# Router steps dealt out singly between low parts, router products one tile later, and idle products in waits: a four-layer gated mixture kernel on one core

## Chip, cores and metric

The kernel runs on one core of a Trainium2 chip. The metric is device time in microseconds (us) of one execution; lower is better.

## What is computed

Four layers update a residual stream x of 8 x 128 tokens by 128 features. Each layer adds a gated cross attention to 77 context tokens and then a gated feed-forward part. Three of the feed-forward parts (layers 0, 1 and 3) are mixtures of 8 experts with the two best experts of each token; layer 2 is a block-quantised feed-forward part. The part of layer 1 that the change touches most, cut from the reference:

```
nx = _ln(x, ln_g, ln_b)
logits = nx @ router_w
probs = jax.nn.softmax(logits, axis=-1)
_, idx = jax.lax.top_k(probs, K)
mask = jnp.sum(jax.nn.one_hot(idx, probs.shape[-1], dtype=probs.dtype), axis=1)
w = probs * mask
w = w / jnp.sum(w, axis=-1, keepdims=True)
h1 = _gelu(jnp.einsum('th,ehf->etf', nx, up_W) + up_b[:, None, :])
...
s0 = _gelu(_ln(jnp.einsum('etf,efg->etg', h1[i0], spec0_W) + spec0_b[:, None, :], ln0_g[:, None, :], ln0_b[:, None, :]))
...
out_e = jnp.einsum('etf,efh->eth', h2, down_W) + down_b[:, None, :]
y = jnp.einsum('eth,te->th', out_e, w) + x
```

Layer 3's mixture is the same without the inner products: relu of an up product, a down product, a softmax over the two kept logits.

## The kernel before

All engines run programs written out by hand, with semaphores between them. The tokens are handled in two halves h of 512. A float32 product is made of three products of rounded parts (`mm3`): an operand is split into a high part (fp32r, by ScalarE) and a low part (the difference, by VectorE for activations, line 1188, and by GpSimd for weights, line 647; the weights' high parts `WH` are ScalarE's, line 737). So every result of an up, inner or turned product in PSUM is read twice by ScalarE (lines 843 and 846) and once by VectorE (`H1l`, `H2l`, the "low parts"), and only after the low part may TensorE use it.

`plan()` writes one list of jobs per mixture (`order[0]`, `order[1]`, `order[3]`); each engine walks that list in `mixture()` and does its share of each job, so the list sets the order on all engines at once. `weave(a, b, ...)` merges lists, list number i starting i rounds later. Up, inner (`spec0`), turned (`turn`), weight (`wgt`) and `spread` results go through a ring of six PSUM banks: TensorE waits, six jobs later, for the reader of that bank (in layer 1 the VectorE low part, in layer 3 ScalarE). Down products accumulate in PS4 and PS5.

Names at the start of layer 1's mixture: four up jobs of expert 0 half 0 (u0 to u3), then four `spec0` jobs (here s0 to s3: a bias row `ROWr` and four groups of three products, one group for each low part of u0 to u3), each followed on VectorE by moments (line 1138) and a scaling `SN` (line 1146). Between them stand held-over steps of the attention part: `late_scale` (ScalarE, line 753, four `XN` tiles), `late_stats` (VectorE), `late_norm` (GpSimd, then ScalarE's four `XM` tiles), and `second`: TensorE turns the second half of XM (line 1504) into XT, ScalarE copies it twice (XT, XTh), VectorE makes XTl (line 1048), and TensorE multiplies it by the router (`logits`, 16 short product instructions of 8 columns, out<-in `PS<-RW,XT`).

The routing itself is VectorE work on 64 numbers per partition (`route`, lines 1065 to 1107): in five parts, part 0 from the logits to the exponent's argument, part 1 the softmax, parts 2 and 3 the two picks, part 4 the weights `WG` and their three bf16 parts `WGS`. `WGS` is turned by TensorE (`wgt`), copied by ScalarE (`WGT`) and spread over the partitions.

After s0 to s3 of the second half come the turned tiles of half 0 (t0 to t3) and of half 1 (r0 to r3), with two up jobs of expert 1 (n0, n1) between them and two more (n2, n3) and the down products of half 1 (e0 to e3) behind them.

`keep_clock(n)` issues n products that nobody reads (`PS<-MB,identb`, 512 columns, bf16).

Of the kernel before, what the change touches and what calls it, by code (L numbers as in the profile page):

```python
# [10 lines left out]
E = 8  # L11
HALF = 512
TH = HALF // S
# [26 lines left out]
def plan():  # L40
# [18 lines left out]
    for p in range(E0P):  # L59
        b = p * U0COLS  # L60
# [38 lines left out]
    route = lambda: [dict(kind="route", part=k) for k in range(5)]  # L99
    second = [dict(kind="second")]  # L100
    order = {0: [], 1: [], 3: []}
# [4 lines left out]
    for n in range(len(x) + 2):  # L106
# [4 lines left out]
        if n == 0:  # L111
            k = route()
            order[0] += k[0:1] + a[0:2] + k[1:2] + a[2:3] + k[2:3] + a[3:4] + k[3:4] + more
        elif n == 1:
            order[0] += a[0:1] + k[4:5] + weave(a[1:], b, c, more)
# [44 lines left out]
    o += u[0:1] + chain("late_scale") + u[1:2] + chain("late_stats") + u[2:4] + chain("late_norm") + s[0:2] + second  # L160
    wq = [dict(kind="quantise", layer=1, i=i, k=k) for i in range(7) for k in range(9)]
    for e in range(E):
# [43 lines left out]
    for n in range(len(x) + 2):  # L206
# [71 lines left out]
def program(nc, a, out):  # L278
# [48 lines left out]
    with ctx:  # L327
# [403 lines left out]
        def _(act):  # L731
# [46 lines left out]
            def mixture(n, layer):  # L778
                for s_ in ORDER[layer]:
                    kind = s_["kind"]  # L780
                    if kind in ("split", "quantise", "down", "down0", "spec0", "spec1b", "weigh") or kind in HELD:
# [15 lines left out]
                    if kind == "route":  # L797
                        if s_["part"] == 0:
                            gate(n)
                        continue  # L800
# [197 lines left out]
        def _(dve):  # L998
# [54 lines left out]
            def route(n, layer, part):  # L1053
# [5 lines left out]
                if part == 0:  # L1059
# [11 lines left out]
                elif part == 1:  # L1071
                    dve.wait_ge(gate_exp, n + 1)
                    if layer < 3:

                        now(v.tensor_reduce(RM[:, 1, :], rt3(1), AX.X, ALU.add))
                        now(v.reciprocal(RM[:, 2, :], RM[:, 1, :]))
                        now(v.tensor_tensor(rt3(2), rt3(1), per_token(RM, 2), ALU.mult))
                elif part in (2, 3):

                    pick = part - 2  # L1080
                    scores = 7 if pick else (9 if layer == 3 else 2)
                    now(v.tensor_reduce(RM[:, 0, :], rt3(scores), AX.X, ALU.max))
                    now(v.tensor_tensor(rt3(3), rt3(scores), per_token(RM, 0), ALU.is_equal))
                    now(v.tensor_tensor(rt(4), rt(3), rev, ALU.mult))
# [932 lines left out]
```

## Time and profile before

| | |
|---|---|
| median of 3 runs (lowest to highest) | 724.83 us (722.32 to 725.20) |
| the profiled execution | 724.68 us |
| its span, first to last instruction | 722.9 us |
| mean granted TensorE clock | 0.964 of full speed |
| busy: TensorE, VectorE, ScalarE, GpSimd | 656.1, 479.8, 436.7, 182.7 us |

The span and the 1.8 us around it make the execution's time. Layer 1's mixture runs from about 181 to 477 us of the span, layer 2 from 477 to 541 us, layer 3's attention from 541 to 604 us and its mixture from 609 to 719 us.

### The profile page before, as it was taken

The page shows a single profiled execution, that of the slowest core. Times are in us where ns is not written, and L with a number is a line of the kernel's source. Part 1 is how long each engine was busy: PE and PEld are TensorE (multiplying, and loading weights), DVE is VectorE, ACT ScalarE, POOL GpSimd, SP SyncE. Part 2 cuts the span into 40 slices and gives each one's busy share as a digit, 9 for nine tenths or more (in the row PEclk, how much of TensorE's full clock was granted, in tenths as well). Part 3 has the DMA queues.
Part 4 walks back from the last instruction along what each step waited for, and adds up shares of the span by engine and source line. Part 5 has one row for each costly group of instructions (what it writes and reads, how often), then busy time and mean ns, then how long its engine had stood idle before and what let it go on. Part 6 is the DMA issues. An engine that isn't in the chain of part 4 may idle for free.

```text
span 722.9 us, 10213 instructions
## 1 busy us (share of the span) xinstructions
PE 656.1 (91%) x3563; PEld 478.1 (66%) x3573; DVE 479.8 (66%) x1093; ACT 436.7 (60%) x820; POOL 182.7 (25%) x215
## 2 busy tenths in 40 slices
PE   4889999998799799998999999997799997889997
PEld 1589996565466677776767667765555665667775
DVE  2477674587447567359657684368975763669996
ACT  4457454877436667668358486655127664877773
POOL 3414000541124033224241512041013001124531
PEclk9789999999789999999999999999999999999999
DMA  5112002020002000022010110010001000110001
GB/s 137 52 31 63 1 1 73 2 88 2 0 2 75 12 15 30 1 73 84 19 59 16 29 60 1 1 47 0 1 1 58 2 3 0 30 46 14 1 0 30
DMA packets 27361, 20.98 MB, mean 29 GB/s; under 512 B 5409, under 2 KB 22571, under 8 KB 27311
## 3 DMA queue, kind: packets, MB, share of 16 engines
q1 hardware_dynamic: 26591, 20.29, 9.3%
q8 instruction: 29, 0.48, 0.3%
q14 instruction: 21, 0.17, 0.1%
q10 hardware_dynamic: 720, 0.04, 0.1%
HBM read 19.80 MB, written 0.52 MB: 28 GB/s over the span
## 4 chain that ended last, share of the span: by engine, by line
PE 62%; DVE 17%; ACT 13%; issue 5%; POOL 2%; DMA 1%; ACTq 0%; DVEq 0%; POOLq 0%
PE PS L1483 54%; ACT PS L846 3%; PE PS L1723 2%; ACT H2h L843 2%; PE PS L1589 2%; ACT H1h L843 2%; ACT XN L753 1%; DVE ST L1020 1%; DVE H2l L1188 1%; DMA GW<-in_L_gate_T 1%; PE PS L1745 1%; PE PS L1504 1%; DVE ATT L1276 1%; ACT WH L737 1%; DVE H1l L1188 1%
## 5 line engine op out<-in xcount | busy, mean ns | idle before, releaser
L647 POOL TENSOR_TENSOR WL<-RAW,WH 128x512 fp32r<-128x512 f32 (+2 forms) x76 | 89.2, 1189 | 147.5 <-ACT WH L737 147.2
L1188 DVE TENSOR_TENSOR H2l<-PS,H2h 128x512 fp32r<-128x512 f32 x72 | 49.3, 689 | 57.9 <-ACT PS L846 57.4
L737 ACT ACTIVATE ATT<-PS 77x512 f32<-77x512 f32 (+5 forms) x92 | 46.7, 533 | 33.6 <-PE PS L1927 15.7
L639 POOL TENSOR_TENSOR RSTD<-VE,MHALF 128x4 f32<-128x4 f32 x18 | 18.6, 1032 | 185.1 <-DVE VE L1030 149.4
L1483 PE MATMUL PS<-XTh,WH 128*128 128x512 f32 x128 | 54.5, 426 | 11.0 <-DVE XTl L1048 4.1
L1483 PE MATMUL PS<-H1h,WH 128*128 128x512 f32 x146 | 60.2, 412 | 2.2 <-DVE H1l L1188 2.2
L665 POOL TENSOR_TENSOR XT<-XT,YW 128x512 f32<-128x512 f32 x24 | 32.2, 1342 | 113.1 <-DVE YW L1125 113.1
L1483 PE MATMUL PS<-H1l,WH 128*128 128x512 f32 x146 | 57.2, 392 | 0.0
L1483 PE MATMUL PS<-H1h,WL 128*128 128x512 f32 x146 | 57.1, 391 | 0.0
L1483 PE MATMUL PS<-XTl,WH 128*128 128x512 f32 x128 | 52.6, 411 | 0.0
L1483 PE MATMUL PS<-XTh,WL 128*128 128x512 f32 x128 | 52.6, 411 | 0.0
L1483 PE MATMUL PS<-H2h,WH 128*128 128x512 f32 (+1 forms) x108 | 48.5, 449 | 2.9 <-DVE H2l L1188 2.2
L1268 DVE TENSOR_REDUCE MX<-PS 128x4 f32<-128x308 f32 x64 | 30.2, 474 | 31.1 <-PE PS L1483 30.7
L843 ACT ACTIVATE H1h<-PS,UB 128x512 fp32r<-128x512 f32 x48 | 33.9, 707 | 26.3 <-PE PS L1483 26.1
L1483 PE MATMUL PS<-MB,identb 128*128 128x512 bf16 (+1 forms) x192 | 48.4, 369 | 0.9 <-issue 0.5
L1188 DVE TENSOR_TENSOR H1l<-PS,H1h 128x512 fp32r<-128x512 f32 x48 | 32.9, 689 | 19.7 <-ACT PS L846 19.4
L846 ACT ACTIVATE PS<-PS,UB 128x512 f32<-128x512 f32 x64 | 44.1, 688 | 0.0
L846 ACT ACTIVATE G<-PS,FB 128x512 f32<-128x512 f32 x64 | 42.6, 704 | 2.0 <-PE PS L1483 0.9
L843 ACT ACTIVATE H2h<-PS,SB 128x512 fp32r<-128x512 f32 x24 | 16.5, 689 | 44.0 <-PE PS L1483 44.0
L1483 PE MATMUL PS<-H2l,WH 128*128 128x512 f32 (+1 forms) x108 | 42.5, 394 | 0.0
L1483 PE MATMUL PS<-H2h,WL 128*128 128x512 f32 (+1 forms) x108 | 42.4, 393 | 0.0
L737 ACT ACTIVATE WH<-RAW 128x512 fp32r<-128x512 f32 (+2 forms) x76 | 41.5, 589 | 0.0
(254 smaller groups left out, 1651.0 us busy)
## 6 DMA issues: line engine op xcount, KB each, us to landing
RAW<-in_L_ffn_spec_W SPq DMA_DIRECT2D x4, 1024.0 KB, 5.5
RAW<-in_L_ffn_w SPq DMA_DIRECT2D x16, 256.0 KB, 3.0
RAW<-in_L_ffn_up_W SPq DMA_DIRECT2D x8, 256.0 KB, 2.7
RAW<-in_L_ffn_down_W SPq DMA_DIRECT2D x8, 256.0 KB, 3.4
RAW<-in_L_ffn_spec1a_W SPq DMA_DIRECT2D x2, 512.0 KB, 4.3
RAW<-in_L_ffn_spec1b_W SPq DMA_DIRECT2D x2, 512.0 KB, 5.6
RAW<-in_L_ffn_wg SPq DMA_DIRECT2D x4, 176.0 KB, 2.6
RAW<-in_L_ffn_wu SPq DMA_DIRECT2D x4, 176.0 KB, 2.7
```

What stands on the lines that cost most here:

```text
L639: step(g.tensor_tensor(RSTD[:, c], VE[:, c], MHALF[:, c], ALU.pow))
L647: g.tensor_tensor(lo, RAW[0:r["rows"], r["raw"] + s["c0"]:r["raw"] + s["c1"]], hi.bitcast(fp32), ALU.subtract).then_inc(lo_done, 1)
L665: g.tensor_tensor(y, y, YW[:, (d % 2) * HALF:(d % 2 + 1) * HALF], ALU.add).then_inc(y_added, 1)
L737: return s.activation(o, i, ACT.Copy)
L753: s.activation(dst[:, t, :], src[:, t, :], ACT.Identity, scale=RSTD[:, t:t + 1], bias=NMR[:, t:t + 1]).then_inc(xn_ready, 1)
L843: s.activation(HID[s_["buf"]][0][:, i * HALF:(i + 1) * HALF], bank[:, :], func, bias=bias, scale=scale)
L846: s.activation(full, bank[:, :], func, bias=bias, scale=scale).then_inc(act_freed, 1)
L1188: v.tensor_tensor(lo, full, hi.bitcast(fp32), ALU.subtract).then_inc(split_done, 1)
L1268: v.tensor_reduce(MX[:, (g % 4) * GH:(g % 4 + 1) * GH], bank(g), AX.X, ALU.max).then_inc(max_done, 1)
L1483: return t_.matmul(o, l, r, start=start, stop=stop)
L1589: last = t_.transpose(o[0:rows, t * S:(t + 1) * S], SN[:, s["slot"], at:at + rows], ident[:, :])
L1723: last = t_.transpose(PS[3 + g % 2][0:KC, m * S:(m + 1) * S], group(PB, g)[:, m * KC:(m + 1) * KC], ident[:, :])
```

## The change

The routing is cut into single steps k = 0 to 25 instead of five parts, and `dealt(items, more, per)` puts `per` of them behind each job. In layer 0 the slices give the same VectorE order as before. In layer 1 the steps go behind the s, t, weight and r jobs, two at a time, then one at a time; in layer 3 behind the up jobs and the jobs of the next round, three at a time. `late_scale` stands two up jobs later; the router products are a job of their own (`scores`), one `spec0` tile behind the turning. Layer 3 puts the second half's turning and its copies ahead of the weight splits of that round, and drops an empty list from every `weave` of layer 3, so that down products and weight splits start one round earlier. Idle products are added in layer 1 (7, before the last group of s0), in layer 3 (6, before the router products) and in layer 2 (9 instead of 8 around the stream products, with half of the context products moved behind the turning; 12, 12, 14, 18 instead of 10, 6, 10, 18 in the feed-forward part).

```
-    route = lambda: [dict(kind="route", part=k) for k in range(5)]
+    route = lambda layer: [dict(kind="route", k=k) for k in range(26)
+                           if not (layer == 0 and k >= 22 or layer == 3 and k in (2, 3))]
     second = [dict(kind="second")]
+    scores = [dict(kind="scores")]
+
+    def dealt(items, more, per):
+
+        out = []
+        for s in items:
+            out.append(s)
+            out += more[:per]
+            more = more[per:]
+        return out, more
...
-            k = route()
-            order[0] += k[0:1] + a[0:2] + k[1:2] + a[2:3] + k[2:3] + a[3:4] + k[3:4] + more
+            k = route(0)
+            order[0] += k[0:1] + a[0:2] + k[1:4] + a[2:3] + k[4:11] + a[3:4] + k[11:16] + more
...
-    o += u[0:1] + chain("late_scale") + u[1:2] + chain("late_stats") + u[2:4] + chain("late_norm") + s[0:2] + second
+    o += u[0:3] + chain("late_scale") + u[3:4] + chain("late_stats", "late_norm") + s[0:2] + second + s[2:3] + scores
...
-            o += weave(s[2:] if e == 0 else spec("spec0", 0, TH), up(e, 1), new[:4])
-            k = route() if e == 0 else []
+            o += weave(s[3:] if e == 0 else spec("spec0", 0, TH), up(e, 1), new[:4])
+            k = route(1) if e == 0 else []
             o += k[0:1]
-            o += weave(spec("spec0", 1, TH), spec("turn", 0, 4, buf=2, hi="act"), new[4:], k[1:])
-            o += nxt[:1] + weave(spec("turn", 1, 4, buf=3, hi="act"), down(e, 0), nxt[1:2])
+            u, k = dealt(weave(spec("spec0", 1, TH), spec("turn", 0, 4, buf=2, hi="act"), new[4:]), k[1:], 2)
+            o += u
+            u, k = dealt(nxt[:1] + weave(spec("turn", 1, 4, buf=3, hi="act"), down(e, 0), nxt[1:2]), k, 1)
+            o += u + k
             o += weave(nxt[2:], down(e, 1))
...
-        order[3] += weave(a, {1: route()[1:3], 2: route()[3:]}.get(n, []), c, more)
         if n == 0:
-            order[3] += second + route()[0:1]
+            r = route(3)
+            order[3] += a + second + scores + more
+        elif n == 1:
+            order[3] += r[0:1] + a[0:2] + r[1:3] + a[2:3] + r[3:5] + a[3:4] + r[5:7]
+        elif n == 2:
+            a, r = dealt(weave(a, c, more), r[7:], 3)
+            order[3] += a + r
+        else:
+            order[3] += weave(a, c, more)
...
+                    if kind == "scores":
+                        k, w = (3, RW1) if layer == 1 else (7, RW3)
+                        if layer == 3:
+                            keep_clock(6, PS[4])
                         logits(n, w[:, :], k)
                         continue
...
+                            if e == 0 and h == 0 and i == 0 and f == nf - 1:
+                                keep_clock(7, PS[4])
...
             context_part(0)
+            keep_clock(7)
+            turn(4, *normed(5, XN), halves=(0,))
             context_part(1)
-            keep_clock(4)
-            turn(4, *normed(5, XN), halves=(0,))
-            keep_clock(4)
+            keep_clock(2)
             stream_part(0)
...
-                keep_clock((10, 6, 10, 18)[p])
+                keep_clock((12, 12, 14, 18)[p])
```

The first place is the start of layer 1's mixture on ScalarE. Before, the four `XN` tiles (`late_scale`) stand behind the first up job:

```order
L843 ACTIVATE H1h<-PS,UB 128x512
L846 ACTIVATE PS<-PS,UB 128x512
L753 ACTIVATE XN<-X,NMR,RSTD 128x128 x4
L843 ACTIVATE H1h<-PS,UB 128x512
L846 ACTIVATE PS<-PS,UB 128x512
```

Now they stand behind the third:

```order
L863 ACTIVATE H1h<-PS,UB 128x512
L866 ACTIVATE PS<-PS,UB 128x512
L863 ACTIVATE H1h<-PS,UB 128x512
L866 ACTIVATE PS<-PS,UB 128x512
L863 ACTIVATE H1h<-PS,UB 128x512
L866 ACTIVATE PS<-PS,UB 128x512
L773 ACTIVATE XN<-X,NMR,RSTD 128x128 x4
```

Two up results are read two jobs earlier, and the four tiles come behind them. On TensorE at the same place the turning, the router products and s2 stood like this before:

```order
L1504 MATMUL PS<-ident,XM 128x128 x4
L1483 MATMUL PS<-RW,XT 128x8 x8
L1483 MATMUL PS<-ROWr,onesr 128x512
L1483 MATMUL PS<-WH,H1h 128x512
L1483 MATMUL PS<-WL,H1h 128x512
```

Now, with the seven idle products ahead of the last group of s0, and the router products behind s2:

```order
L1518 MATMUL PS<-MB,identb 128x512 x7
L1518 MATMUL PS<-WH,H1h 128x512
...
L1539 MATMUL PS<-ident,XM 128x128 x4
L1518 MATMUL PS<-ROWr,onesr 128x512
...
L1518 MATMUL PS<-RW,XT 128x8 x8
L1518 MATMUL PS<-ROWr,onesr 128x512
```

The second place is VectorE in layer 1, from the low part of t2 to that of n0 (the one `H1l` row). Before, 22 of the 25 routing steps behind the exponent stand between t3's low part and n0's (the first two and the last two are shown):

```order
L1188 TENSOR_TENSOR H2l<-PS,H2h 128x512
L1082 TENSOR_REDUCE RM<-RT 128x8
L1083 TENSOR_TENSOR RT<-RT,RM 128x64
...
L1106 CAST WGS<-RT 128x8x8
L1107 TENSOR_TENSOR WGS<-RT,WGS 128x8x8
L1188 TENSOR_TENSOR H1l<-PS,H1h 128x512
L1188 TENSOR_TENSOR H2l<-PS,H2h 128x512 x3
```

Now the low parts of t2, t3 and n0 stand between them, and thirteen of the steps are ahead of t2:

```order
L1223 TENSOR_TENSOR H2l<-PS,H2h 128x512
L1115 TENSOR_TENSOR RT<-RT,RM 128x64
L1119 TENSOR_TENSOR RT<-RT 128x64
L1121 TENSOR_TENSOR RT<-RT 128x64
L1123 TENSOR_REDUCE RM<-RT 128x8
L1223 TENSOR_TENSOR H2l<-PS,H2h 128x512
L1127 RECIPROCAL RM<-RM 128x8
L1129 TENSOR_TENSOR RT<-RT,RM 128x64
L1223 TENSOR_TENSOR H1l<-PS,H1h 128x512
L1131 TENSOR_SCALAR WG<-RT,TG 128x64
```

Two steps stand between t3's low part and n0's where there were 22. The third place is ScalarE at the start of layer 3's mixture. Before, two weight splits stand ahead of the copies of the second half's turned tiles:

```order
L846 ACTIVATE G<-PS,FB 128x512
L737 ACTIVATE WH<-RAW 128x512 x2
L737 ACTIVATE XT<-PS 128x512
L737 ACTIVATE XTh<-PS 128x512
L927 ACTIVATE RT<-RT 128x64
```

Now behind them:

```order
L866 ACTIVATE G<-PS,FB 128x512
L757 ACTIVATE XT<-PS 128x512
L757 ACTIVATE XTh<-PS 128x512
L757 ACTIVATE WH<-RAW 128x512 x2
L947 ACTIVATE RT<-RT 128x64
```

The copies are issued two splits earlier, and so the splits' high parts, which GpSimd waits for, two copies later.

## Rows read from the trace of the kernel before

**Rows 1.** Windows: length, busy us of PE, PEld, DVE, ACT, POOL; clock; DMA.
```profile
180.80:189.40 8.60, 5.18 (x22) 3.31 (x20) 4.53 (x19) 6.35 (x12) 1.21 (x2) 1.00 0.00 1
189.40:199.60 10.20, 9.14 (x20) 6.14 (x20) 3.57 (x12) 2.44 (x6) 1.75 (x3) 0.50 0.00 0
203.00:206.40 3.40, 3.40 (x10) 2.65 (x9) 0.17 (x1) 0.00 (x0) 0.00 (x0) 0.50 0.00 0
240.60:244.00 3.40, 3.08 (x7) 2.48 (x8) 3.32 (x7) 1.99 (x4) 0.00 (x0) 0.50 0.00 0
482.90:486.30 3.40, 3.38 (x10) 1.80 (x11) 0.31 (x1) 2.83 (x8) 3.32 (x5) 0.50 0.00 0
```

**Rows 2.** Timeline, start of layer 1: start, length, engine, [idle before <-releaser].
```profile
182.37 0.65 ACT L846 ACTIVATE PS<-PS,UB 128x512 f32<-128x512 f32 x1
185.13 1.65 ACT L753 ACTIVATE XN<-X,NMR,RSTD 128x128 f32<-128x128 f32 x4 [2.10 <-POOL NMR L640]
188.66 0.50 PE L1483 MATMUL PS<-WH,H1h 128*128 128x512 f32 x1 [3.26 <-DVE H1l L1188]
190.78 0.80 PE L1483 MATMUL PS<-WH,H1h 128*128 128x512 f32 x1 [1.05 <-DVE H1l L1188]
191.47 1.65 ACT L753 ACTIVATE XM<-XN,NMR,RSTD 128x128 f32<-128x128 f32 x4 [1.28 <-POOL NMR L640]
200.08 2.09 PE L1483 MATMUL PS<-RW,XT 128*128 128x8 f32 x16
207.07 0.49 PE L1483 MATMUL PS<-ROWr,onesr 33*128 33x512 f32 x1
210.36 0.40 PE L1483 MATMUL PS<-XTh,WH 128*128 128x512 f32 x1
```

**Rows 3.** Timeline, layer 1 around the routing.
```profile
234.03 0.68 ACT L846 ACTIVATE PS<-PS,UB 128x512 f32<-128x512 f32 x1
234.32 0.21 DVE L1082 TENSOR_REDUCE RM<-RT 128x8 f32<-128x64 f32 x1
239.95 0.23 DVE L1107 TENSOR_TENSOR WGS<-RT,WGS 128x64 bf16<-128x64 f32 x1
240.37 0.84 ACT L846 ACTIVATE PS<-PS,LB,LG 128x512 f32<-128x512 f32 x1
240.92 0.77 PE L1483 MATMUL PS<-XTh,WH 128*128 128x512 f32 x1 [3.01 <-DVE H1l L1188]
248.10 0.60 PE L1483 MATMUL PS<-WGT,PICK 96*128 96x512 bf16 x2 [0.95 <-ACT WGT L737]
```

**Rows 4.** Timeline, layer 2.
```profile
484.58 0.60 ACT L737 ACTIVATE XT<-PS 128x512 f32<-128x512 f32 x1 [0.57 <-PE PS L1504]
487.35 0.75 DVE L1238 SCALAR_TENSOR_TENSOR X<-PS,TG,X 128x512 f32<-128x512 f32 x1 [4.14 <-PE PS L1483]
519.04 0.87 PE L1927 MATMUL PS<-ident,ATT 128*128 128x128 f32 x6 [1.62 <-DVE ATT L1355]
```

**Rows 5.** Timeline, start of layer 3's mixture.
```profile
616.02 1.18 ACT L737 ACTIVATE WH<-RAW 128x512 fp32r<-128x512 f32 x2
616.76 2.49 POOL L647 TENSOR_TENSOR WL<-RAW,WH 128x512 fp32r<-128x512 f32 x2 [10.69 <-ACT WH L737]
618.21 1.59 DVE L1048 TENSOR_TENSOR XTl<-XT,XTh 128x512 fp32r<-128x512 f32 x1 [1.32 <-ACT XTh L737]
619.90 0.76 PE L1483 MATMUL PS<-XTh,WH 128*128 128x512 f32 x1 [1.10 <-POOL WL L647]
638.71 0.61 PE L1483 MATMUL PS<-WGT,PICK 96*128 96x512 bf16 x2 [2.27 <-ACT WGT L737]
```

**Rows 6.** Line 1188 on DVE: nanoseconds, least, median, most; first and last start.
```profile
L1188 DVE TENSOR_TENSOR H1l<-PS,H1h x48: 678/691/694, 183.7 to 449.2; 128x512 fp32r<-128x512 f32 x48
L1188 DVE TENSOR_TENSOR H1l<-G,H1h x32: 677/692/1783, 612.6 to 700.6; 128x512 fp32r<-128x512 f32 x32
```

**Rows 7.** Windows, layer 3's mixture in full flow, columns as in Rows 1.
```profile
656.00:700.00 44.00, 44.00 (x190) 34.15 (x189) 43.49 (x53) 34.12 (x59) 21.43 (x14) 1.00 0.00 1
```

More of the change, by code:

```diff
@@ L111, in plan @@
         if n == 0:
-            k = route()
-            order[0] += k[0:1] + a[0:2] + k[1:2] + a[2:3] + k[2:3] + a[3:4] + k[3:4] + more
+            k = route(0)
+            order[0] += k[0:1] + a[0:2] + k[1:4] + a[2:3] + k[4:11] + a[3:4] + k[11:16] + more
         elif n == 1:
-            order[0] += a[0:1] + k[4:5] + weave(a[1:], b, c, more)
+            order[0] += a[0:1] + k[16:] + weave(a[1:], b, c, more)
         elif n == E0P + 2:
@@ L780, in mixture @@
                     kind = s_["kind"]
-                    if kind in ("split", "quantise", "down", "down0", "spec0", "spec1b", "weigh") or kind in HELD:
+                    if kind in ("split", "quantise", "scores", "down", "down0", "spec0", "spec1b", "weigh") or kind in HELD:
                         if kind == "y_copy":
@@ L797, in mixture @@
                     if kind == "route":
-                        if s_["part"] == 0:
+                        if s_["k"] == 0:
                             gate(n)
@@ L1051, in per_token, with route @@
                 return m[:, row, :].rearrange("p (t o) -> p t o", o=1).to_broadcast([128, B, E])
-            def route(n, layer, part):
+            def route(n, layer, k):
                 rt = lambda i: RT[:, i, :]
@@ L1058, in route @@
                 prob = 1 if layer == 3 else 2
-                if part == 0:
+                third = lambda k: WGS[:, :, 32 * k:32 * k + E]
+                wg = WG[:, :].rearrange("p (t e) -> p t e", e=E)
+                if k == 0:
                     dve.wait_ge(v1_ready, 1)
@@ L1070, in route @@
                     v.tensor_tensor(rt3(0), rt3(9), per_token(RM, 0), ALU.subtract).then_inc(dif_ready, 1)
-                elif part == 1:
+                elif k == 1:
                     dve.wait_ge(gate_exp, n + 1)
@@ L1095, in route @@
                     now(v.reciprocal(RM[:, 1, :], RM[:, 0, :]))
+                elif k == 20:
                     now(v.tensor_tensor(rt3(8), rt3(8), per_token(RM, 1), ALU.mult))
+                elif k == 21:
                     v.tensor_scalar(WG[:, :], rt(8), tg(4 + layer), None, ALU.mult).then_inc(wg_ready, 1)
                     dve.wait_ge(wg_ready, n + 1)
[L1099 to L1107 removed]
+                elif k == 22:
+                    now(v.memset(WGS[:, :, :], 0.0))
+                    now(v.tensor_copy(third(0), wg))
+                elif k == 23:
+                    now(v.tensor_tensor(rt3(8), wg, third(0), ALU.subtract))
+                elif k == 24:
+                    now(v.tensor_copy(third(1), rt3(8)))
+                else:
+                    v.tensor_tensor(third(2), rt3(8), third(1), ALU.subtract).then_inc(wgs_ready, 1)
             def mixture(n, layer):
@@ L1153, in mixture @@
                     if kind == "route":
-                        route(n, layer, s["part"])
+                        route(n, layer, s["k"])
                     elif kind == "second":
```

43 lines of the change are left out of this document (23 added, 20 removed).

## The prediction, as put on record before the changed kernel ran

> **What bounds the kernel now.** I read the windows first, then the waits in the timeline, place by place. TensorE is busy 656.1 of 722.9 us, so time is to be had only where it waits, or where it runs at 1.2 GHz instead of 2.4. The windows show such stretches [rows 1]: 189.4 to 199.6, 203.0 to 206.4, 240.6 to 244.0 and 482.9 to 486.3 stand at 0.50. The reader is to see that each follows a wait or a stretch of short products, and that a stretch full of products (9.14 busy of 10.20) still runs at half rate once it has fallen.
>
> The waits, in order of time. In layer 1, TensorE has the first group of s0 done and waits 3.26 us for the low part of u1, then 1.05 for those of u2 and u3 [rows 2]. The releaser is VectorE, but the late one is ScalarE: behind u0 (its last read starts 182.37) it stands at the four `XN` tiles until NMR is there, 185.13, and is done with them at 186.78; only then does it read u1. Around the routing, TensorE waits 3.01 us for n0's low part, at 240.92. ScalarE had n0 read at 234.03 + 0.68 = 234.71, so VectorE is late by itself: 22 routing steps run from 234.32 to 240.18 ahead of it [rows 3]. That is 5.86 us, 0.266 us a step. In layer 3's mixture TensorE waits for XTl, which VectorE made in 1.59 us, from 618.21 to 619.80, though the row of TensorE names GpSimd [rows 5]. In the flow of layer 3 TensorE is busy all 44.00 us [rows 7], and in layer 2's feed-forward part the waits before line 1927 are for VectorE's quantising [rows 4].
>
> **The change, term by term.** A product group of 512 columns goes by every 0.23 us at full clock. I take a whole `spec0` tile from rows: 207.07 to 210.36, 3.29 us for 13 products [rows 2].
>
> *A, start of layer 1.* ScalarE reads 512 columns every 0.59 us (two in 1.18 [rows 5]), so an up result takes 1.2. u0 is done at 183.0, then u1 at 184.2 and u2 at 185.3; NMR comes at 185.1, so the tiles move by only 0.2 (185.3 to 186.9), and u3 is read at 188.1. VectorE's low parts (0.69 each [rows 6]) are then there at about 185.0, 186.0 and, for u3, 188.8. TensorE does groups two and three of s0 by 186.8, the seven idle products (7 x 0.23 = 1.6) by 188.4, and starts the last group at 188.9: 189.6. Then s1 with 3.29: 192.9. The turning needs XM. `late_stats` follows u3's low part, 0.2 later than before, so the XM tiles end at 191.47 + 1.65 + 0.2 = 193.3 and the turning at 193.5 [rows 2]. s2: 196.8, and the router products, 2.0 of their 2.09 behind it: 198.8. At that point the old kernel, with s2 and the router products behind it as well, stood at 207.07. The gain is 8.2 us if the clock stays at 2.4 GHz. Ahead of the fall TensorE was busy 5.18 of 8.60 us, with the 3.26 wait in it [rows 1]; of that wait 0.5 is left, which makes about 7.9, so I expect the long slow stretch gone. But the short slow one, 203.0 to 206.4, came directly behind the turning and the router products, at a time when TensorE had no wait at all. The same products are still issued, so I keep that stretch and charge half of its 3.4 us: **A = -6.5**. Ends: -8.2 without it; -4.2 if the 10.2 us stay slow (s1 6.0 at half rate until 195.5, the turning to 195.7, s2 3.9 slow and 1.2 fast to 200.8, router 202.9).
>
> The Trainium skill bears on this ("TensorE: Matmul & The Clock Gate", Part 4: PE-mode transpose): transposes do not count as busy in the way other products do. By that the fall behind the turning stays; by the row of 203.0 alone it is the router products or the turning. Both say 1.7 us are still paid.
>
> *B, the routing in layer 1.* Thirteen steps move into VectorE's idle time ahead of t2's low part. Six run between t2's and n0's low parts and cost 6 x 0.266 = 1.6 us, against 25 (6.6) before. So n0's low part ends at about 236.3, not 240.8, and TensorE, which began to wait at 240.92 - 3.01 = 237.9, goes on at once, and without the stretch at 0.50 that came of it. What is late next is ScalarE: it reads r3 until 240.37 + 0.84 = 241.2, then n2 and n3 (2 x 1.2), then makes the two WGT copies (1.2): 244.8. The products with WGT start there instead of at 248.10 [rows 3]: **B = -3.3**. Ends: -4.6 (the whole wait and half of 3.4 slow us); -1.0 if routing steps ahead of t0's to t3's low parts hold TensorE's ring.
>
> *C, layer 2.* XT is there at 485.18; the stream products stood behind four idle products at half rate, and their VectorE reader started at 487.35 [rows 4]. Now a half of the context products (1.0) and two idle ones (0.45) stand behind the turning: reader at about 486.75 if the clock is full, -0.6; at half rate about 488.6, +1.3. Whether the granted clock stays is not to be read from these rows, as TensorE is equally busy ahead of it. **C = 0**. The idle products in the feed-forward part lie in waits: six more at line 1927's second wait are 1.4 us in 1.62 [rows 4]; VectorE, which sets the pace there, does not wait for them. If the clock fell there, 12 products would take 5.1 us and be late by about 2.
>
> *D, layer 3's start.* Without the two weight splits (1.18 us [rows 5]) ahead, ScalarE makes XT and XTh by 617.1. GpSimd's low parts of the weights, which ran from 616.76 to 619.25 over XTl, come later, so XTl takes 0.69 and is ready at 617.9 instead of 619.80. The six idle products (1.4) and the router products lie in the old wait (done 617.7). Next up job: 618.0, not 619.90, which is -1.9. Its first three products took half rate (0.76 and so on, where 210.36 has 0.40); at full clock ScalarE has its first result another 0.7 sooner, -2.6. Ahead of the last low part of the third round nine routing steps stand now instead of twelve, 3 x 0.27 more, -3.4. The 2.27 wait for the WGT copies [rows 5], which are ScalarE's, stays. Between these I take **D = -3.0**, ends -1.9 and -3.7.
>
> *The rest.* Layer 0's VectorE order is the same: 0. In layer 3's flow the down products stand one place earlier, but they use low parts two rounds old, and ScalarE's splits only change places: 0.
>
> Sum: -6.5 - 3.3 + 0 - 3.0 = -12.8. From the profiled execution, 724.68 (span 722.9 and 1.8 around it; the median is 724.83, the same within 0.15): 711.9, so **712 us**.
>
> The contention in D is also a rule: the Trainium skill ("GPSIMD Engine Reference", 1. Specifications) lists SBUF access as shared with VectorE, with contention when its instruction has two SBUF inputs. The low parts agree: from PSUM never over 694 ns in 48, from `G` in SBUF up to 1783 [rows 6]. The routing steps have two SBUF inputs as well. So this rule speaks against the change in one respect, the next rival but one.
>
> **Rivals.** *The clock does not hold in layer 1* (0.14). For it: full stretches stayed at 0.50 once [rows 1]; against: the wait that preceded them goes. A is then -4.2: 714.2.
>
> *The waits come back* (0.13): routing steps ahead of low parts delay TensorE's ring in layer 1 (B = -1.0) and the last low part of the third round in layer 3 (nine steps stand ahead of it, D = -1.9): 715.3. For it: each step stands in an in-order queue; against: the steps are the same in sum and only begin earlier.
>
> *Slower: VectorE becomes the bound in layer 3's flow* (0.03). It is busy 43.49 of 44.00 us there [rows 7], with low parts stretched to 1.78 beside GpSimd. Down products earlier and splits between up jobs change which of its instructions meet GpSimd's. The flow is seven pairs of rounds; it has 0.5 us of slack in 44. If in each pair three more of its eight low parts stretch by 1.1 (0.69 to 1.78), that is 3.3 a pair, 23.1 in all, less about 0.9 of slack: 712 + 22.2 = 734. It decides from 2 us a pair on (7 x 2 - 0.9 = 13). Against: the order of VectorE and GpSimd is the same there.
>
> *The skill's rule on the port* (0.08): in layer 3 the last nine steps meet the two low weight parts (2.5 us of GpSimd). They would end 2.5 later and take D to -0.5: 714.5. The page is the one named above, and the rule agrees with the 1.59 of XTl.
>
> *More than forecast* (0.10): the slow stretch behind the router products goes, A -8.2 instead of -6.5, and C at -0.6: 709.7.
>
> **How the numbers follow.** The forecast itself has 0.52, at 710 to 714. The range 707.5 to 717.5 takes in all the best ends together (-8.2 - 4.6 - 0.6 - 3.7 is 707.6) and all rivals but the slower one; it leaves about 0.15 out. A change of 0.5% (3.6 us) is about what a measurement of this kernel can tell from none: under 721.2 is faster. The cases there hold 0.93; 0.04 for two or three terms failing together, 0.03 for the slower rival.
>
> **What would show it.** Right: in layer 1 no wait over 1 us between the first and last group of s0, granted clock 1.00 through s1, 8 us less from u0's first product to s3 give or take 2; no wait for n0's low part, and the products with WGT bounded by ScalarE, 3.3 us earlier; XTl of 0.7 us in layer 3; VectorE's waits none in layer 2's feed-forward part. Wrong: a slow stretch over s1 and s2, waits for `H2l` on TensorE between t0 and r3, any wait of TensorE in layer 3's flow, or new slow stretches elsewhere that give back 1.7 us each.

## The result and the profile after

The changed kernel takes 718.01 us (median of 4, 717.73 to 719.47), the kernel before 724.68 in the same comparison. The ratio is 0.9924, 95% interval 0.9899 to 0.9949: 6.7 us faster, where 12.7 had been forecast, and just outside the forecast's range (707.5 to 717.5). The profiled execution took 719.47 us with a span of 717.7.

The windows of the changed kernel, columns as in [rows 1]:

```profile
186.00:199.00 13.00, 12.64 (x59) 8.61 (x59) 8.38 (x25) 4.48 (x9) 3.34 (x5) 1.00 0.00 0
199.00:202.40 3.40, 3.40 (x9) 2.62 (x10) 0.47 (x1) 0.00 (x0) 0.00 (x0) 0.50 0.00 0
226.30:229.70 3.40, 2.84 (x11) 2.65 (x12) 3.20 (x9) 3.07 (x6) 0.90 (x1) 0.50 0.63 211
328.70:332.10 3.40, 3.40 (x10) 2.63 (x9) 3.16 (x9) 2.38 (x4) 0.85 (x1) 0.50 0.69 231
506.20:509.60 3.40, 3.40 (x14) 3.15 (x15) 3.23 (x6) 0.38 (x2) 0.00 (x0) 0.50 0.02 5
629.10:639.30 10.20, 7.31 (x17) 5.11 (x18) 4.41 (x8) 5.10 (x10) 0.00 (x0) 0.50 0.00 1
```

The 10.2 us at half clock in layer 1 [rows 1] are gone: 186 to 199 us stand at 1.00. But the stretch at 328.7 is new, and in layer 3 there are 10.2 us from 629.1 where the kernel before has 3.4 (from 639.9). In layer 3's flow, 650 to 694 us, TensorE is busy all 44.00 us as in [rows 7], so the rival that made the kernel slower did not come. The timeline of the changed kernel, with the waits in brackets:

```profile
188.17 0.50 PE L1518 MATMUL PS<-WH,H1h 128*128 128x512 f32 x1 [0.18 <-DVE H1l L1223]
198.48 0.49 PE L1518 MATMUL PS<-ROWr,onesr 33*128 33x512 f32 x1
221.46 1.29 POOL L667 TENSOR_TENSOR WL<-RAW,WH 128x512 fp32r<-128x512 f32 x1 [0.60 <-ACT WH L757]
221.69 1.14 DVE L1115 TENSOR_TENSOR RT<-RT,RM 128x64 f32<-128x64 f32 x1
224.23 0.70 DVE L1173 BATCH_NORM_STATS2 ST<-PS 128x6 f32<-128x512 f32 x1
226.86 1.97 PE L1682 MATMUL PS<-ident,SN 128*128 128x128 f32 x8 [2.50 <-DVE SN L1181]
233.49 0.39 PE L1518 MATMUL PS<-XTh,WH 128*128 128x512 f32 x1
328.31 0.50 PE L1518 MATMUL PS<-XTh,WH 128*128 128x512 f32 x1 [2.02 <-POOL WL L667]
611.35 0.69 DVE L1068 TENSOR_TENSOR XTl<-XT,XTh 128x512 fp32r<-128x512 f32 x1 [0.28 <-ACT XTh L757]
627.51 0.65 PE L1518 MATMUL PS<-identb,WGS 128*96 128x128 bf16 x8 [1.05 <-DVE WGS L1142]
630.43 1.03 PE L1518 MATMUL PS<-WGT,PICK 96*128 96x512 bf16 x2 [2.27 <-ACT WGT L757]
635.59 0.77 PE L1518 MATMUL PS<-H2h,WH 128*128 128x512 f32 x1 [1.55 <-DVE XT L1160]
```

The waits for u1 and n0 are gone. In their place stand 2.50 us for the scaled tile SN, and in layer 3 1.55 us for VectorE's weighing into XT (the step that reads a finished down product out of PS4 and multiplies it by the gate weights). At these two places the timeline of the kernel before has 1.09 and 0.38:

```profile
232.47 1.09 PE L1640 MATMUL PS<-ident,SN 128*128 128x128 f32 x8 [1.09 <-DVE SN L1146]
...
642.92 0.67 PE L1483 MATMUL PS<-H2h,WH 128*128 128x512 f32 x1 [0.38 <-DVE XT L1125]
```

Since the first product of layer 1's mixture starts anywhere from 179.9 to 182.7 us in these traces, whatever was edited, the traces are compared by the lengths between five marks on TensorE: u0's first product (M0), the first `spec0` product of the second half (M1), the WGT products of layer 1 (M2), the first up product of layer 3 (M3), the WGT products of layer 3 (M4), and the end of TensorE's last instruction (M5). The starts are read from each run's timeline and subtracted; us:

```
run                   M0-M1  M1-M2   M2-M3  M3-M4  M4-M5   median  ratio to before (95%)
before                32.47  34.83  361.55  29.06  80.69
the change            26.06  32.95  364.51  26.73  83.73   718.01  0.9924 (0.9899-0.9949)
l3_list_back          26.07  32.97  364.51  26.13  81.90   716.98  0.9893 (0.9867-0.9920)
l1_route_old          26.07  34.80  362.94  26.74  83.71   720.46  0.9934 (0.9909-0.9958)
l1_no_idle            25.57  33.23  362.90  26.65  82.75   718.11  0.9912 (0.9889-0.9935)
l2_old                26.13  33.09  363.27  26.63  81.87   718.18  0.9913 (0.9891-0.9936)
before_late_scale     28.81  34.99  361.60  29.06  80.74   719.02  0.9926 (0.9906-0.9945)
list_back_no_idle     25.58  33.18  362.85  26.25  81.49   716.52  0.9880 (0.9858-0.9903)
plus_no_idle_l3       28.66  33.21  362.92  27.29  80.48   716.98  0.9894 (0.9873-0.9916)
plus_deal_later       25.57  31.96  362.72  24.61  80.48   715.22  0.9864 (0.9833-0.9895)
before_A_alone        26.07  34.94  361.61  29.07  80.67   718.54  0.9936 (0.9912-0.9959)
before_B_alone        32.49  33.25  363.20  29.07  80.70   724.27  1.0013 (0.9997-1.0029)
before_D_alone        32.54  34.90  361.54  26.00  80.70   721.10  0.9963 (0.9947-0.9979)
before_list_dropped   29.73  34.92  361.55  28.82  82.75   727.52  1.0055 (1.0035-1.0075)
before_B_shifted      32.44  34.65  361.63  29.05  80.73   724.54  1.0008 (0.9993-1.0024)
before_B_later        32.72  31.96  363.10  29.31  80.50   720.86  0.9966 (0.9944-0.9989)
parts_best            25.58  31.94  361.67  26.00  80.66   712.18  0.9850 (0.9827-0.9874)
```

The ratios are each to the kernel before as it ran in the same comparison. Its median was 724.68 us there for the change, 724.76 for the next eight lines, 723.67 for the four from `before_A_alone` on and 723.93 for the last three, so medians of different groups are not to be subtracted to a few tenths. The lengths are those of one profiled execution each. One of the nine executions of `l1_route_old` took 816.09 us at a granted clock of 0.754 and is left out of its ratio.

By the first two lines the change gained 6.4 (A), 1.9 (B) and 2.3 us (D), and lost 3.0 between M2 and M3 and 3.0 behind M4.

### The profile page after: what moved, and what is told of

Its sections match the earlier page's. It is cut to its first block, busy times and chain, and to the rows that moved or that the text cites. A ratio compares the mean times of both kernels' runs of the same rounds, so it can differ in the third digit from the quotient of the medians.

```text
span 717.7 us, 10278 instructions
## 1 busy us (share of the span) xinstructions
PE 660.7 (92%) x3588; PEld 480.7 (67%) x3599; DVE 481.4 (67%) x1093; ACT 438.7 (61%) x820; POOL 183.1 (26%) x215
## 4 chain that ended last, share of the span: by engine, by line
PE 64%; DVE 16%; ACT 13%; issue 4%; POOL 2%; DMA 1%; ACTq 0%; DVEq 0%; POOLq 0%
PE PS L1518 55%; ACT PS L866 3%; PE PS L1765 3%; ACT H2h L863 2%; PE PS L1629 2%; ACT H1h L863 2%; ACT XN L773 1%; DVE H2l L1223 1%; PE PS L1787 1%; DVE ST L1040 1%; PE PS L1682 1%; DMA GW<-in_L_gate_T 1%; DVE QS L1363 1%; PE PS L1539 1%; ACT ATT L757 1%
## 5 line engine op out<-in xcount | busy, mean ns | idle before, releaser
L1518 PE MATMUL PS<-MB,identb 128*128 128x512 bf16 (+1 forms) x217 | 54.4, 372 | 1.0 <-issue 0.5
L1223 DVE TENSOR_TENSOR H1l<-PS,H1h 128x512 fp32r<-128x512 f32 x48 | 32.9, 689 | 18.5 <-ACT PS L866 18.3
L1518 PEld LDWEIGHTS PS<-MB,identb 128*128 128x128 bf16 x228 | 20.2, 101 | 34.4 <-issue 20.4
```

The costliest lines, as they stand in the source:

```text
L1223: v.tensor_tensor(lo, full, hi.bitcast(fp32), ALU.subtract).then_inc(split_done, 1)
L1518: return t_.matmul(o, l, r, start=start, stop=stop)
```

## The experiments

**Undoing one edit of the change.** `l3_list_back` puts layer 3's empty list back:

```diff
-            a, r = dealt(weave(a, c, more), r[7:], 3)
+            a, r = dealt(weave(a, [], c, more), r[7:], 3)
...
-            order[3] += weave(a, c, more)
+            order[3] += weave(a, [], c, more)
```

> The changed kernel with one edit undone: the empty list is back in layer 3's weaves, so that down products and weight splits start one round later, as before. Theory 1 (the earlier first down product waits for the weighing of the accumulator it writes over, and the wait and the low clock with it give back what the start of layer 3 gained): the wait of 1.55 us on DVE XT is gone or under 0.5, the stretch at clock 0.50 in layer 3's third round is 3.4 us instead of 10.2, and the time is 2.5 to 3 us under the changed kernel, 715.2 (before is 724.7). Rival (the low clock comes from the 2.27 us wait for the WGT copies alone, and falls wherever that stands): the stretch stays 10.2 us long, and the time falls by at most 1 us, to 717 or more.

716.98. The wait for XT is 0.28 us, as theory 1 said, but the stretch at half clock is 6.8 us long, not 3.4, and 1.0 us was gained by the median where 2.8 was expected; that is the time the rival named, and the two intervals overlap. In the profiled runs M3 to M4 is 0.6 and M4 to M5 1.8 shorter. Theory 1 has the direction, not the size, and the 0.28 is no proof of its cause, as `plus_deal_later` shows below.

`l1_route_old` puts layer 1's routing back into the four blocks of before:

```diff
-            u, k = dealt(weave(spec("spec0", 1, TH), spec("turn", 0, 4, buf=2, hi="act"), new[4:]), k[1:], 2)
-            o += u
-            u, k = dealt(nxt[:1] + weave(spec("turn", 1, 4, buf=3, hi="act"), down(e, 0), nxt[1:2]), k, 1)
-            o += u + k
+            parts = [k[1:4], k[4:11], k[11:16], k[16:]] if k else []
+            for s in weave(spec("spec0", 1, TH), spec("turn", 0, 4, buf=2, hi="act"), new[4:], parts):
+                o += s if isinstance(s, list) else [s]
+            o += nxt[:1] + weave(spec("turn", 1, 4, buf=3, hi="act"), down(e, 0), nxt[1:2])
```

> The changed kernel with layer 1's routing in the four blocks of before. Theory 1 (dealing out is worth little there, 1.8 us, since a step that meets GpSimd's weight split takes 1.14 us instead of 0.22 and moves the scaling SN of the last tile): 719.8, with a wait of about 3 us for n0's low part and none over 1.5 us at the turned tiles. Rival (it is worth the 3.3 us forecast and the loss is elsewhere): 721.3. Second rival (it is worth nothing; either way one wait and one stretch at clock 0.50): 718.

M1 to M2 is 34.80, 1.85 us more than with the dealing, and the 3.01 us wait for n0 is back. But M2 to M3 is 1.6 us shorter: no stretch at half clock stands behind the wait for WL. 720.46 lies between theory 1 and the rival, but its runs (716.07 to 722.32, the one of 816.09 apart) take in those of the change, and the ratios can't be told apart. In the traces B's gain is real and smaller than forecast, and something later takes most of it.

`l1_no_idle` drops the seven idle products:

```diff
-                            if e == 0 and h == 0 and i == 0 and f == nf - 1:
-                                keep_clock(7, PS[4])
```

> The changed kernel without the seven idle products ahead of the last group of s0 in layer 1. Theory 1 (the shorter wait is what keeps the clock, the idle products do nothing): same time as the changed kernel, 718, clock 1.00 from 186 to 198 us. Rival (they keep the clock): TensorE waits 1.6 us there, a stretch at 0.50 of 3.4 to 10.2 us follows through s1 and s2, and the time is 719.7 to 722.5.

The total stays, 718.11, yet not by theory 1's way: TensorE waits 1.72 us, and a stretch of 3.4 us comes at 190.1, but the one of 199.0 does not. M0 to M1 is 0.5 us shorter than with them. The idle products only moved where the clock falls. (Of four later runs with the same start of layer 1 three show 25.6 us for that part and one 28.66, with 6.8 us of half clock from 189.9 and 3.4 more behind the router products, so the fall can also be longer.)

`l2_old` undoes part C:

```diff
             context_part(0)
-            keep_clock(7)
-            turn(4, *normed(5, XN), halves=(0,))
             context_part(1)
-            keep_clock(2)
+            keep_clock(4)
+            turn(4, *normed(5, XN), halves=(0,))
+            keep_clock(4)
...
-                keep_clock((12, 12, 14, 18)[p])
+                keep_clock((10, 6, 10, 18)[p])
```

> The changed kernel with layer 2 as before: both halves of the context products ahead of the turning, 4 and 4 idle products, and 10, 6, 10, 18 in the feed-forward part. Theory 1 (the order behind the turning costs 1.1 us at the half clock: two idle products and half of the context products stand ahead of the stream products, and six more idle ones behind them): 716.9, and VectorE's second addition to X comes 3.6 us behind its first instead of 4.7. Rival (the place of the low clock decides, not the order): within 0.5 us of the changed kernel, 718.

The second addition to X comes 3.6 us behind the first, as theory 1 said (481.68 and 485.26; in the changed kernel 480.25 and 484.97). The time does not follow: 718.18. The rival holds in the median, though the profiled run is 1.2 us shorter between M2 and M3 than that of the change.

**A first combination.** `before_late_scale` is the kernel before with one line:

```diff
-    o += u[0:1] + chain("late_scale") + u[1:2] + chain("late_stats") + u[2:4] + chain("late_norm") + s[0:2] + second
+    o += u[0:3] + chain("late_scale") + u[3:4] + chain("late_stats", "late_norm") + s[0:2] + second
```

> The kernel before with one edit of the change: late_scale two up jobs later (and late_stats with late_norm behind the fourth). No idle products, router products where they were, routing in blocks. Theory 1 (the shorter wait alone keeps TensorE's clock through s1 and s2): from u0's first product to the second half's first products 26 to 27 us instead of 32.5, one stretch of 3.4 us at clock 0.50 there instead of 10.2 and 3.4, and 718.5. Rival (the router products behind s2 are needed too): the stretch of 10.2 us stays and only the waits go, 721 to 722.

719.02, ratio 0.9926: this line alone gives as much as the whole change (0.9924). Theory 1 holds for the size; in the profiled run, which is the longest of the five (720.87), the stretch is 6.8 us long with 3.4 behind the router products (28.81, not 26 to 27).

`list_back_no_idle` is `l3_list_back` without the seven idle products.

> The changed kernel with the empty list back in layer 3 and without layer 1's seven idle products. Theory 1 (the two act in stages far apart and add up: -1.0 as measured for the list, -0.5 for layer 1's start by the stretch from u0 to the second half, 25.6 us against 26.1): 716.5. Rival (a removal of 0.5 us moves everything behind it against the clock's stretches, so that sums do not hold): anything from 715 to 719, with the stretches at 0.50 at other places than in the two runs apart.

716.52, as theory 1 said.

`plus_no_idle_l3` is that without the six idle products ahead of layer 3's router products:

```diff
-                        if layer == 3:
-                            keep_clock(6, PS[4])
```

> As list_back_no_idle, and without the six idle products ahead of layer 3's router products. Theory 1 (they do nothing for the clock, and lie in a wait): the same time within 0.5 us. Rival (they keep the clock): the stretch at 0.50 around the router products grows by 3.4 us or more and costs 1 to 2 us between the first up product and the WGT products of layer 3 (26.1 to 26.7 us so far).

716.98, within 0.5 us, as theory 1 said. But in the profiled run M3 to M4 is 1.0 longer and 6.8 us of half clock stand at the router products (from 613.2), where the run without this edit has none; that is what the rival named. The runs of 716.5 to 718.9 overlap those without the edit (714.5 to 717.3). Whether the six idle products help is not settled.

`plus_deal_later` deals layer 1's steps otherwise:

```diff
-            u, k = dealt(weave(spec("spec0", 1, TH), spec("turn", 0, 4, buf=2, hi="act"), new[4:]), k[1:], 2)
-            o += u
-            u, k = dealt(nxt[:1] + weave(spec("turn", 1, 4, buf=3, hi="act"), down(e, 0), nxt[1:2]), k, 1)
+            k = k[1:]
+            for s in weave(spec("spec0", 1, TH), spec("turn", 0, 4, buf=2, hi="act"), new[4:]):
+                o.append(s)
+                if s["kind"] != "split" and (s["kind"], s["i"]) != ("turn", 1):
+                    o += k[:2]
+                    k = k[2:]
+            u, k = dealt(nxt[:1] + weave(spec("turn", 1, 4, buf=3, hi="act"), down(e, 0), nxt[1:2]), k, 2)
             o += u + k
```

> As list_back_no_idle, with layer 1's routing dealt out otherwise: no steps behind t1 and behind weight splits, so that the moments of the last spec0 tile stand four to six steps earlier on VectorE, and two steps instead of one behind the jobs that follow t3. Theory 1 (the steps ahead of the last tile's moments, one of them stretched to 1.14 us beside GpSimd, cause TensorE's 2.50 us wait for SN and the low clock with it): the wait is 1.1 us as in the kernel before, and the time from the second half's first product to the WGT products is 31.3 us instead of 33.0; 715. Rival (the steps only move: n0's or r0's low part is late instead): the wait for SN is shorter and waits of the same sum stand at the H1l and H2l behind it; 33 us, 716.5.

M1 to M2 is 31.96, 1.2 us shorter than in `list_back_no_idle`, and no stretch stands there. 715.22, as theory 1 said, but with runs from 711.7 to 719.1. The waits went the rival's way: 1.73 us for SN instead of 2.50 (not 1.1), and a new one of 0.83 for a low part behind it, 2.56 together. So the 1.2 us are the stretch at half clock that did not come, not a shorter wait. TensorE's timeline:

```profile
226.51 1.09 PE L1684 MATMUL PS<-ident,SN 128*128 128x128 f32 x8 [1.73 <-DVE SN L1185]
236.26 0.50 PE L1522 MATMUL PS<-H2h,WH 128*128 128x512 f32 x1 [0.83 <-DVE H2l L1227]
630.14 0.47 PE L1522 MATMUL PS<-H2h,WH 128*128 128x512 f32 x1 [1.49 <-DVE XT L1164]
```

The last row stands in layer 3, where this kernel has the empty list: the wait for XT is 1.49 us and not 0.28. It is as long in `plus_no_idle_l3`, which has the list too, and in `before_B_later`, whose layer 3 is that of the kernel before. What the three share is full clock between the WGT products and this one. The product starts 4.20 us behind the WGT products here, 4.21 in the kernel before and 4.20 in `before_list_dropped`: in these three VectorE's weighing sets that time, with and without the list. With a stretch at half clock there, TensorE's three groups of up products fill the wait; at full clock they leave 1.49 us.

**One part at a time on the kernel before.** `before_A_alone` has `late_scale`, the idle products and `scores` as in the change, `before_B_alone` the dealing in layer 1, `before_D_alone` layer 3's start with the empty list kept; their edits are those lines of the change, with the routing steps and the router products that are not under test in their old places. `before_list_dropped` drops the empty list, with the routing's blocks still behind the second and third up job (`b0`, `b1`):

```diff
-        order[3] += weave(a, {1: route()[1:3], 2: route()[3:]}.get(n, []), c, more)
...
+            order[3] += weave(a, c, more) + second + scores + r[0:1]
...
+            order[3] += flat(weave([a[0], a[1:2] + b0, a[2:3] + b1, a[3]], c, more))
+        else:
+            order[3] += weave(a, c, more)
```

> The kernel before with part A alone, as in the change: late_scale later, the seven idle products, router products behind s2. Theory 1 (A is worth the 6.4 us that the start of layer 1 shows in the changed kernel): from u0 to the second half's first products 26.1 us instead of 32.5, nothing else moves, 718.3. Rival (stretches at clock 0.50 elsewhere move with it and give part back): 26.1 us there too, but 720 or more.

> The kernel before with part B alone: layer 1's routing dealt out as in the change. Theory 1 (it gains 1.9 us up to the WGT products, and a stretch at 0.50 behind the 2.02 us wait for WL, near 340 us, gives 1.5 back): 724.4. Rival (that stretch has nothing to do with it and does not come): 722.9. The forecast's own term, -3.3, would give 721.5.

> The kernel before with part D alone, the empty list kept: in layer 3 the turning's copies ahead of the weight splits, six idle products, routing dealt out. Theory 1 (2.5 us are gained up to the WGT products, and 1.2 us are lost behind them, since WGS comes 0.7 us later against TensorE's work and the stretch at 0.50 there is 6.8 us instead of 3.4): 723.5. Rival (the gain stays): 26.1 to 26.7 us instead of 29.1 up to the WGT products and 80.7 us from there to the end as before, 722.0.

> The kernel before with the empty list of layer 3's weaves dropped and nothing else: down products and weight splits one round earlier. Theory 1 (the first down product over PS4 waits for VectorE's weighing, 1.2 us, whatever the rest does): 726.0, with a wait of 1.5 us on DVE XT in the third round. Rival (there is no wait without part D, the term is 0 as forecast): 724.8.

A: 6.4 us in its place and nothing elsewhere, 718.54: theory 1 for the stretch; the ratio makes it 4.6 us of the total (3.0 to 6.4). B: 1.6 us gained, 1.65 lost between M2 and M3, 724.27, no change that can be told: theory 1. D: 3.1 us gained and none given back (M4 to M5 80.70 as before), 721.10: the rival holds and my theory falls. The list: 727.52, slower, with an interval clear of 1. That is theory 1's direction, and more than it said. TensorE's timeline there, and at the same place of `before_D_alone`:

```profile
641.33 0.47 PE L1517 MATMUL PS<-H2h,WH 128*128 128x512 f32 x1 [2.18 <-DVE XT L1159]
```

```profile
639.29 0.47 PE L1518 MATMUL PS<-H2h,WH 128*128 128x512 f32 x1 [0.27 <-DVE XT L1160]
```

2.18 us of wait against 0.27. Two things are in this difference. The first down product that writes PS4 again stands one job earlier, while VectorE's weighing of what PS4 holds comes when it came; and `before_D_alone` has 3.4 us at half clock ahead of that product (from 635.8), which fill its wait. Against 1.49, the same wait with the list and at full clock, the list costs 0.69 us, one group of three up products that now stands behind the wait instead of in it. M4 to M5 lost 2.1 us by the table; the other 1.4 are not shown singly, but they fit the stretch at half clock, which here falls behind the wait, from 642.1, on products without a gap. In its stages the profiled run of `before_list_dropped` shows 1.8 us of loss from M3 on; it is the fastest of seven, so the rest of the median's 3.9 us is not in it.

**Is it the dealing, or the place?** Seven profiled runs with the dealing of the change, `before_B_alone` among them, have a stretch at half clock behind the 2.02 us wait for WL; the six without dealing have the same wait and no stretch (nor have the three with the later dealing). `before_B_shifted` keeps the dealing and moves all that follows by 1.6 us:

```diff
                     elif kind == "wgt":
...
                         o = ring(j)
+                        if layer == 1 and h == 0:
+                            keep_clock(7, o)
```

> As before_B_alone, with seven idle products of 512 columns (1.6 us) on TensorE ahead of layer 1's WGS product, which puts everything behind them back to where it stood in the kernel before. Theory 1 (the place in time decides): no stretch at 0.50 behind the 2.02 us wait for WL, 245.8 us from the WGT products to layer 2's weight turning, and the same total as before_B_alone, 724, since 1.6 us are put in and 1.6 us do not come. Rival (the dealing is the cause): the stretch stays, 247.4 us there, total 725.8.

The wait for WL and the clock behind it, first in `before_B_alone` (timeline and window; the stretch begins at 338.1, 0.4 us into the window, so that the mean is over 0.50):

```profile
337.57 0.50 PE L1516 MATMUL PS<-XTh,WH 128*128 128x512 f32 x1 [2.02 <-POOL WL L665]
```

```profile
337.70:341.10 3.40, 3.40 (x9) 2.66 (x10) 3.15 (x8) 2.26 (x4) 1.11 (x1) 0.56 0.72 202
```

and in `before_B_shifted`:

```profile
336.55 0.49 PE L1516 MATMUL PS<-XTh,WH 128*128 128x512 f32 x1 [2.02 <-POOL WL L665]
```

```profile
336.50:343.30 6.80, 6.75 (x27) 4.93 (x28) 6.46 (x14) 5.25 (x9) 2.56 (x2) 1.00 0.71 231
```

The same wait, the same products behind it, and half clock against 1.00. M2 to M3 is 1.6 us shorter (361.63 against 363.20), and the total, 724.54, is that of `before_B_alone` (724.27) with 1.6 us of idle work put in. So not the dealing but the place in time decides, as theory 1 said, as far as one trace of each can show it.

`before_B_later` is the kernel before with the dealing of `plus_deal_later`.

> The kernel before with layer 1's routing dealt out as in plus_deal_later and nothing else. Theory 1 (this dealing gains 2.9 us up to the WGT products, as that run showed, and no stretch comes behind the wait for WL): 721.0 to 721.8. Rival (the gain of plus_deal_later was a lucky place of the clock's stretches): 1.6 us up to the WGT products, 723 or more.

720.86 (717.3 to 725.3): M1 to M2 is 31.96, 2.9 us shorter, and nothing falls behind the wait for WL. In the profiled run, 723.88 and among the longer ones, a stretch of 6.8 us at the start of layer 2 takes 1.6 back. Theory 1 holds in the median; what a single execution keeps varies.

`parts_best` puts together what was found: `late_scale` and `scores` as in the change without the seven idle products, the later dealing, layer 3's start with the list kept, layer 2 as before.

> Late_scale later and router products behind s2 without the seven idle products, the later dealing in layer 1, layer 3's start as in the change with the empty list kept, layer 2 as before. Theory 1 (the parts add up: -6.2, -2.9 and -2.9 against 724.7): 712.7. Rival (what one part gains the clock's stretches take back, as in plus_deal_later, whose runs spread over 7 us): 715, with single runs from 711 to 719.

712.18 (711.67 to 716.36), ratio 0.9850 (0.9827 to 0.9874): faster than the change, whose interval begins at 0.9899, and near theory 1's sum. In layer 3 the wait for XT is hidden again, by 3.4 us at half clock from 628.4 (timeline; the mean granted clock of the run is 0.982, and 0.964 in the change):

```profile
631.64 0.54 PE L1522 MATMUL PS<-H2h,WH 128*128 128x512 f32 x1 [0.28 <-DVE XT L1164]
```

## Why the prediction missed

**A, forecast -6.5, measured -6.4** (table; `before_A_alone` the same in its place, and -4.6 by its ratio, with its interval just short of 6.5). The steps held: from u0's first product to s3's start it is 18.3 us where it was 26.3, so 8.0 us less where 8.2 had been worked out (s3 starts at 198.48, forecast 198.8), the long slow stretch is gone, and the one of 3.4 us behind the turning and the router products stays, at 199.0 instead of 203.0. The share of half of it that I charged, 1.7, was about right. The idle products do not belong to the cause: without them the total is the same. Nor does the move of the router products, as far as the totals tell: `before_late_scale` has 0.9926 and `before_A_alone` 0.9936.

**B, forecast -3.3, measured -1.9 here and 0 alone.** The wait for n0 goes, as forecast. The step that failed is "Thirteen steps move into VectorE's idle time ahead of t2's low part". That time is not all idle: a turned tile's low part and three steps stand ahead of the last tile's moments (224.23), and one step behind the tile before met GpSimd's weight split and took 1.14 us instead of 0.23. So SN is late, and TensorE waits 2.50 us where it waited 1.09. These 1.4 us are as much as the miss up to the WGT products (3.3 forecast, 1.9 measured). I had weighed the contention in layer 3 only. The Trainium skill ("GPSIMD Engine Reference", 1. Specifications) lists contention with GpSimd for VectorE instructions with two SBUF inputs, and the 1.14 agrees: the step reads two tiles in SBUF while GpSimd's weight split runs (221.46 to 222.75). With the three steps gone and a step of 1.14 us still there (229.18), SN's wait in `before_B_later` is 1.73. That kernel gains 2.9 up to the WGT products, but its waits there are as long in sum as B's (1.73 and 0.80): it gains more because no stretch at half clock comes. The forecast had counted on that for B too, and it did not happen: instead of the stretch at 240.6 there is one at 226.3. So the wait and the clock both bear on the miss, and the runs do not part their shares. The second loss is the stretch at half clock behind the wait for WL near 330 us, 1.3 to 1.65 us, which no step of mine looked at, since nothing changes there but the hour.

**C, forecast 0 (-0.6 to +1.3), measured about 0 to +1.2.** M2 to M3 is 1.2 us longer in the profiled run of the change than in that of `l2_old`, and 506.2 to 509.6 stands at half clock. `l1_no_idle` has part C and no stretch there, and undoing C does not change the median. Inside the range named; whether C costs anything is open.

**D, forecast -3.0, measured -2.3 here and -3.1 alone.** XTl takes 0.69 as forecast, and at the start of layer 3 the missing 0.7 lies in the stretch of half clock around M3, 6.8 us instead of 3.4. The rival of the two low weight parts, 2.5 us later, did not come: in `before_D_alone` one step beside GpSimd's split takes 0.93 us (628.93), and 26.00 stands against 29.06 all the same.

**The rest, forecast 0, measured +3.0 behind M4.** The step that failed is "the down products stand one place earlier, but they use low parts two rounds old". True of what they read. What they write was not asked: PS4 must first be weighed out by VectorE, whose time does not move, so that the job that was pulled ahead waits and a group of up products that had stood in the wait stands behind it, 0.69 us. TensorE waits 1.05, 2.27 and 1.55 us here, and stands at half clock for 10.2 us instead of 3.4. Of the 3.0 us, 1.8 go when the list is put back, and 1.2 stay with a stretch of 6.8 us; by the medians the list costs 1.0 here and, by its ratio, 4.0 (2.5 to 5.4) alone. So the direction is shown, and the size beyond the 0.69 is not: it goes with where the stretches at half clock fall, and how it splits stays open. What the forecast put at nothing besides is the clock elsewhere: "or new slow stretches elsewhere that give back 1.7 us each" was written as a sign of being wrong and had no term in the sum.

Sum of the table's differences: -6.4 - 1.9 + 3.0 - 2.3 + 3.0, and 0.6 by an earlier M0, give -5.2, the difference of the two spans (722.9 and 717.7); the medians differ by 6.7. A was sized right in its place, and D alone (-3.1). The gap of 7.6 us to the forecast, by the spans, is 3.0 between M2 and M3, 3.0 behind M4, B's 1.4, D's 0.7 and A's 0.1, less the 0.6 of M0. The chances do not add up either: the cases as listed make 1.00 with the forecast and leave nothing for the 0.04 of several terms failing together, which is what happened. Of the rivals, "the waits come back" named the mechanism of B, with its place wrong.

## What to carry over

When an order is changed by a place, ask of each moved job what it reads and also what it writes over: a bank is free only when its last reader has been through it. "Idle time" of an engine ahead of a late result has to be read row by row up to that result, with what a small step costs beside another engine's use of the same memory. A wait that is gone from a row need not be gone: at half clock TensorE's own products can fill it (0.28 us in one kernel here, 1.49 in another with the same order there), so waits are compared only at the same clock. Cut a change of many parts into single ones before believing in any: here one line gave as much as the whole, what the others gained was lost again, and the good ones together are worth twice the whole (ratio 0.9850 against 0.9924).

## What the runs showed of the hardware

- The same wait of 2.02 us with the same work around it is followed by 3.4 us at half clock in one kernel (`before_B_alone`, from 338.1) and by 1.00 in another (`before_B_shifted`), which differs in 1.6 us of idle products some 90 us ahead. What an edit gains in one place can so be taken back 90 us later, in a stretch that it does not touch. The forecast, made from the trace of before, foresaw no such stretch.
- Idle products do not always hold the clock. With seven of them, TensorE's wait in s0 was 0.18 us, and the clock fell behind the router products (199.0); without them the wait was 1.72 us, and it fell at 190.1 instead. One stretch of 3.4 us in either of these two traces.
- A VectorE step on 64 numbers a partition, 0.23 us by its median of six, took 1.14 us beside a GpSimd weight split of 1.29 us, as much as five steps (line 1115 of the changed kernel, 221.69). Another, line 1121, took 1.21 us at 622.49 beside the split of 622.25.
- One kernel can spread by 7 us from execution to execution: `plus_deal_later` ran from 711.7 to 719.1, with mean granted clocks of 0.985 and 0.973 at the two ends and 0.968 in a run between them, so the mean clock alone does not order them.
